# A fused recurrent-attention and expert layer on one Trainium2 core: the first eight steps' log rows come from TensorE, and the last half expert's rows are written over batches finished without them

## The reference, cut to what matters

```python
xn = _layernorm(x)                                   # x: 8 batches x 512 tokens x 256
s  = _L0_attn_ref(xn, ...)
g  = _silu(_L0_ffn_ref(xn, ...))
return x + s * g

# attention, for each batch, chunks of 128 tokens, 16 heads of 16
q, k, v = silu(xn @ Wq.T), silu(xn @ Wk.T), xn @ Wv.T
lf = cumsum(log_sigmoid(xn @ Wf.T + delta))          # within each chunk: "lb" below
o_inter = (q * exp(lb)) @ S
A = (q @ k.T) * exp(where(tril, lb_i - lb_j, -inf))
o = o_inter + A @ v
S = exp(tot) * S + (k * exp(tot - lb)).T @ v
s = (o * rsqrt(mean(o * o) + 1e-6) * norm_weight) @ Wo.T

# experts: 8 experts, each takes its top 128 tokens of every batch
gating, idx = top_k(softmax(xn @ gate_w.T).T, 128)
h = silu(x_in @ w_gate.T) * (x_in @ w_up.T)
out.at[idx].add(gating * (h @ w_down.T))
```

## Time and profile before

| | us |
|---|---|
| median of 3 runs (837.76 to 840.04) | 838.71 |
| the profiled execution, its own time | 838.68 |
| its span in the profile | 836.9 |
| PE busy | 783.8 (94%) |
| DVE, ACT, POOL busy | 541.6, 508.7, 413.8 |

### The profile page before, as it was taken

The page is one execution under the profiler, slowest core; times in us unless marked ns, Lnnn a source line. Parts: engine busy times, 40 slices in busy tenths (PEclk is TensorE's granted clock), DMA queues, the critical chain, the costliest instruction groups (busy, mean ns, idle before and its releaser), DMA issues.

```text
span 836.9 us, 17482 instructions
## 1 busy us (share of the span) xinstructions
PE 783.8 (94%) x6460; PEld 678.3 (81%) x6460; DVE 541.6 (65%) x1024; ACT 508.7 (61%) x1184; POOL 413.8 (49%) x362
## 2 busy tenths in 40 slices
PE   7638999999999999999999999999999999999990
PEld 5526788888888888888888888888888888888880
DVE  6885756666566675666556675576556675565567
ACT  5695755766466665666466655665566655655455
POOL 7767636464255616463355626463364625471311
PEclk9778999999999999999999999999999999999995
DMA  8289898676567857676566757576667758670788
GB/s 279 93 284 226 302 372 214 171 197 196 150 155 192 178 178 165 160 196 193 162 148 193 187 167 161 165 195 190 177 145 189 192 165 230 167 179 16 219 254 288
DMA packets 137637, 160.85 MB, mean 192 GB/s; under 512 B 11856, under 2 KB 108624, under 8 KB 137552
## 3 DMA queue, kind: packets, MB, share of 16 engines
q1 hardware_dynamic: 124832, 142.91, 56.3%
q0 software_dynamic: 12288, 16.79, 12.5%
q10 hardware_dynamic: 432, 0.04, 0.0%
HBM read 117.48 MB, written 42.21 MB: 191 GB/s over the span
## 4 chain that ended last, share of the span: by engine, by line
PE 87%; DMA 3%; SPq 2%; POOL 1%; DVE 1%; issue 1%; ACT 1%; ACTq 0%; DVEq 0%; POOLq 0%
PE y_ps L1699 22%; PE g_ps L1666 21%; PE up_ps L1666 21%; PE m_ps L1542 5%; PE a_ps L1614 4%; PE o_ps L1650 3%; PE m_ps L1596 3%; PE m_ps L1560 2%; PE m_ps L1589 2%; DMA qk_dram<-qk_r 1%; PE o_ps L1639 1%; PE m_ps L1570 1%; SPq L739 1%; DMA ffn_dram<-y_sb,idx_all 1%; DMA w_raw<-w_experts 1%; SPq L695 1%
## 5 line engine op out<-in xcount | busy, mean ns | idle before, releaser
L1666 PE MATMUL up_ps<-xgt,w_r 128*128 128x512 f32 (+1 forms) x792 | 205.8, 395 | 0.0
L1699 PE MATMUL y_ps<-w_r,hid_r 128*128 128x256 f32 x1536 | 205.1, 282 | 0.7 <-DVE hid_r L1493 0.7
L1666 PE MATMUL g_ps<-xgt,w_r 128*128 128x512 f32 (+1 forms) x792 | 201.0, 389 | 3.3 <-ACT xgt L1046 1.8
L1699 PEld LDWEIGHTS y_ps<-w_r,hid_r 128*128 128x128 f32 x1536 | 192.5, 190 | 1.4 <-DVE hid_r L1493 1.0
L1467 DVE SCALAR_TENSOR_TENSOR sg<-sg,g_ps 128x512 f32<-128x512 f32 x123 | 84.2, 684 | 159.9 <-ACT sg L1211 159.9
L887 POOL TENSOR_TENSOR w_r<-w_raw,w_r 128x768 fp32r<-128x768 f32 x64 | 123.1, 1925 | 103.3 <-ACT w_r L1111 103.1
L1666 PEld LDWEIGHTS up_ps<-xgt,w_r 128*128 128x128 f32 x792 | 140.2, 188 | 26.8
L1666 PEld LDWEIGHTS g_ps<-xgt,w_r 128*128 128x128 f32 x792 | 137.7, 189 | 26.1 <-issue 3.6
L1211 ACT ACTIVATE sg<-g_ps 128x512 f32<-128x512 f32 (+1 forms) x132 | 77.1, 584 | 117.0 <-PE g_ps L1666 116.5
L916 POOL DMA_INDIRECT ffn_dram<-y_sb,idx_all x64 | 102.9, 1608 | 64.5 <-DVE y_sb L1369 49.0
L882 POOL TENSOR_SCALAR_AFFINE_SELECT lb_row<-lb_row 128x1024 f32<-128x1024 f32 x62 | 75.8, 1233 | 84.0 <-DMA lb_row<-lb_tiles 83.8
(11 more groups left out here) (246 smaller groups left out, 1021.2 us busy)
## 6 DMA issues: line engine op xcount, KB each, us to landing
lb_row<-lb_tiles SPq DMA_DIRECT2D x62, 512.0 KB, 4.5
w_raw<-w_experts SPq DMA_DIRECT2D x64, 384.0 KB, 3.7
qk_dram<-qk_r SPq DMA_DIRECT2D x32, 512.0 KB, 4.5
k_st<-qk_dram SPq DMA_DIRECT2D x96, 128.0 KB, 3.6
arena<-qk_dram SPq DMA_DIRECT2D x192, 64.0 KB, 3.0
x_all<-x SPq DMA_DIRECT2D x8, 512.0 KB, 9.7
xn_dram<-x_all SPq DMA_DIRECT2D x8, 512.0 KB, 6.6
e_row<-lb_tiles SPq DMA_DIRECT2D x64, 64.0 KB
```

What stands on the lines that cost most here:

```text
L1666: mm = pe.matmul(bank[:, 0:width(n)], w_r[:, m, a, at:at + P], xgt[:, b, k, tokens], start=(j == 0 and k == 0), stop=(j == len(passes) - 1 ...
L1699: mm = pe.matmul(y_ps[:, j, :], hid_r[p][:, a, (j - first_tile) * P:(j - first_tile + 1) * P], w_r[:, m, b, DOWN:DOWN + D], start=(m == 0 ...
```

## The change

It changes both ends of the program. The middle of the loop stays as it is.

**At the start.** The logs of steps 0 to 7 no longer go through DRAM: `spread_logs(t)` on PE writes them into PSUM, one product of an identity with a masked tile (512 columns, with -1e30 above the diagonal) and four fp32 products of 128 columns that spread one row of `lbt` each. `decays(t)` reads PSUM for `t < 8`. `spread_rows(kk)` does the same for batch 0's query rows (four products each), and `rows(0)` moves ahead of the loop. Gone are `load_lb(0..3)`, `mask(0..3)` and `load_rows(0)`. The job ("kt", 0, 0) moves into the loop (`u = 1`), the loads of weight blocks 2 and 3 ahead of SP's loop, `scaled(4)` from ACT to POOL, `out_weights`, two decays and the keys' load forward. ACT makes three constant tiles at the start of `normalise`.

**At the end.** The last half expert is not scattered. Its rows are gathered: of x, of f as the other 15 groups left it, of s (now stored by token) and of r (now also stored to DRAM, as single floats). `row_total` adds the gated result to the gathered f, ACT takes the SiLU, `row_result` finishes the row, and `write_rows` writes it over the row in `out`, after the store of that batch has landed. So batches 4 to 7 are finished first (`FINISH`), beside PE's last steps, and then 0 to 3. The root is taken on DVE alone from a bit-shifted seed with three Newton steps, in two parts (28 tiles, then 4); ACT switches to its SiLU table at `u = TS`.

```diff
-    FIRST = [("k", 0, 0), ("k", 0, 1), ("q", 0, 0), ("q", 0, 1), ("v", 0, 0), ("v", 0, 1), ("kt", 0, 0)]
+    FIRST = [("k", 0, 0), ("k", 0, 1), ("q", 0, 0), ("q", 0, 1), ("v", 0, 0), ("v", 0, 1)]
...
+    FINISH = (4, 5, 6, 7, 0, 1, 2, 3)
+    SOON = 3
+    R_PARTS = (slice(0, (B - 1) * TPB), slice((B - 1) * TPB, NT))
+    ACT_LATE = {TS: ((4, "silu", 0), (4, "silu", 1)), TS + 1: ((5, "weigh", 0), (5, "silu", 0)),
+                TS + 2: ((5, "silu", 1), (6, "weigh", 0)), TS + 3: ((6, "silu", 0), (6, "silu", 1)),
+                TS + 4: ((7, "silu", 0),), TS + 5: ((7, "silu", 1),), TS + 6: ((0, "silu", 0),), TS + 7: ((0, "silu", 1),),
+                TS + 8: ((1, "silu", 0),), TS + 9: ((0, "row", 0), (1, "row", 0)), TS + 10: ((1, "silu", 1),),
+                TS + 11: ((2, "silu", 0),), TS + 12: ((2, "silu", 1), (3, "silu", 0), (3, "silu", 1))}
+    LATE_BETWEEN = {TS + 2: (4, 512, 1024), TS + 5: (6, 0, 256), TS + 6: (6, 512, 768), TS + 7: (6, 768, 1024),
+                    TS + 8: (7, 0, 256), TS + 9: (7, 256, 512), TS + 10: (7, 512, 768), TS + 11: (7, 768, 1024)}
+    DVE_LATE = {TS: ((4, "weigh", 0, 512),), TS + 1: ((4, "weigh", 512, 1024), (4, "add", 0, 512)),
+                TS + 2: ((5, "scaled", 0, 512),), TS + 3: ((5, "scaled", 512, 1024), (5, "add", 0, 1024), (6, "scaled", 0, 512)),
+                TS + 4: ((6, "scaled", 512, 1024),), TS + 5: ((6, "add", 256, 512),), TS + 6: ((7, "weigh", 0, 512),),
+                TS + 7: ((7, "weigh", 512, 1024),), TS + 9: ((0, "rows", 0, 0),), TS + 10: ((1, "rows", 0, 0),),
+                TS + 11: ((0, "weigh", 0, 512),), TS + 12: ((0, "weigh", 512, 1024),)}
...
 sync:
+                def store_r(part):
+                    sp.wait_ge(r_step, R_STEPS * (part + 1))
+                    tiles = R_PARTS[part]
+                    sp.dma_start(r_dram.rearrange("(t p) o -> p (t o)", p=P)[:, tiles], r1[:, tiles],
+                                 allow_slow_non_contiguous=True).then_inc(r_out[part], 16)
...
                 for n in range(2):
                     sp.wait_ge(qk_out[n], 16)
+                load_keys(0)
                 store_part(0, 3)
-                load_keys(0)
+                store_xn(2)
+                load_stacks(0)
                 store_xn(3)
-                load_stacks(0)
+                load_stacks(1)
                 store_lb(1)
-                load_stacks(1)
-                load_rows(0)
+                store_xn(4)
+                sp.wait_ge(d_out, 32)
+                sp.wait_ge(row_exp, 1)
                 for n in range(4, 6):
                     load_lb(n)
+                for n in range(2, 4):
+                    load_weights(n)
...
+                    if u == TS - 4:
+                        store_r(0)
+                    if u == TS - 2:
+                        sp.wait_ge(scattered, 16 * TPB * (2 * E - 2))
+                        for n in FINISH[:SOON]:
+                            fetch_f(n)
...
 gpsimd:
+                def write_rows(t):
+                    pool.wait_ge(o_pair[t // 2], 32)
+                    pool.wait_ge(row_done, 2 * t + 2)
+                    pool.indirect_dma_start(
+                        out=out[:, :], out_offset=bass.IndirectOffsetOnAxis(ap=idx_all[:, E - 1, TPB + t:TPB + t + 1], axis=0),
+                        in_=row_f[t], in_offset=None).then_inc(rows_out, 16)
...
+                    if u == TS - 6:
+                        for t in range(TPB):
+                            gather_rows(row_x, x, t, row_in_soon)
+                    if u == TS - 4:
+                        pool.wait_ge(scattered, 16 * TPB * (2 * E - 2))
+                        for t in range(TPB):
+                            gather_rows(row_f, ffn_dram, t, row_in_soon)
+                    if u == TS - 2:
+                        ...
+                        pool.wait_ge(r_out[0], 16)
+                        for t in range(TPB - 1):
+                            gather_rows(row_s, s_dram[0:(B - 1) * N, :], t, row_in_soon)
+                            gather_rows(row_r, r_dram[0:(B - 1) * N, :], t, row_in_soon)
+                    if u == TS + 4:
+                        ...
+                        gather_rows(row_s, s_dram, TPB - 1, row_in_late)
+                        gather_rows(row_r, r_dram, TPB - 1, row_in_late)
+                    if u == TS + 9:
+                        write_rows(0)
+                        write_rows(1)
...
 scalar:
                 sums(0)
+                act.wait_ge(attn_in[2], 32)
+                out_weights()
+                evacuate(FIRST[3])
                 split(FIRST[2])
-                evacuate(FIRST[3])
-                scaled(2)
+                gates_ratio(1)
+                decays(0)
                 split(FIRST[3])
+                decays(1)
                 evacuate(FIRST[4])
                 evacuate(FIRST[5])
+                scaled(2)
                 scaled(3)
-                act.wait_ge(attn_in[2], 32)
-                out_weights()
-                decays(0)
-                decays(1)
+                decays(2)
+                decays(3)
                 sums(1)
-                for t in range(2, DECS):
-                    decays(t)
+                decays(4)
+                rows(0)
...
 vector:
+                def row_total(t):
+                    dve.wait_ge(dn_done, XQ + MID if t < 2 else XS)
+                    dve.scalar_tensor_tensor(out=row_f[t], in0=y_ps[:, t, :], scalar=gate_all[:, E - 1, TPB + t:TPB + t + 1],
+                                             in1=row_f[t], op0=ALU.mult, op1=ALU.add).then_inc(row_sum, 1)
+                def row_result(t):
+                    dve.wait_ge(row_silu, t + 1)
+                    dve.scalar_tensor_tensor(out=row_f[t], in0=row_f[t], scalar=row_r[t], in1=row_s[t],
+                                             op0=ALU.mult, op1=ALU.mult).then_inc(row_done, 1)
+                    dve.tensor_tensor(row_f[t], row_f[t], row_x[t], ALU.add).then_inc(row_done, 1)
...
-                gated(2 * E - 1, range(2, TPB))
-                add_tokens(1)
-                ...
+                row_total(2)
+                row_total(3)
+                add_tokens(0, slice(0, 512))
+                row_result(2)
+                row_result(3)
+                add_tokens(0, slice(512, 1024))
+                for f in (1, 2):
+                    for h in range(2):
+                        weigh(f, slice(h * 512, (h + 1) * 512))
                     add_tokens(f)
                 for h in range(2):
                     at = slice(h * 512, (h + 1) * 512)
-                    weigh_scaled(B - 1, at)
-                    add_tokens(B - 1, at)
+                    weigh_scaled(3, at)
+                    add_tokens(3, at)
...
 tensor:
+                def spread_logs(t):
+                    if t == 0:
+                        pe.wait_ge(soft, 6)
+                        pe.wait_ge(lb_turned, 2)
+                    if t >= 2:
+                        pe.wait_ge(e_done, t - 1)
+                    pe.matmul(first_logs(t)[:, :], one_r, shut_r.unsqueeze(1).broadcast_to([P, G4, P]), start=True, stop=False,
+                              skip_group_check=True)
+                    for j in range(G4):
+                        r = t * G4 + j
+                        mm = pe.matmul(first_logs(t)[:, j * P:(j + 1) * P], ident[:, r:r + 1].broadcast_to([P, P]),
+                                       lbt[0][:, 0, :], start=False, stop=True, skip_group_check=True)
+                    mm.then_inc(spread_done, 1)
...
                 sums(0)
+                spread_logs(0)
+                spread_logs(1)
                 make(FIRST[4])
                 make(FIRST[5])
-                make(FIRST[6])
+                spread_logs(2)
+                spread_logs(3)
                 sums(1)
+                spread_logs(4)
+                for kk in range(KD):
+                    spread_rows(kk)
+                for t in range(5, FREE):
+                    spread_logs(t)
```

More of the change, by code:

```diff
@@ L37 @@
 TOPK_ROUND = 8
+MASKED = -1e30
 def f32(ap):
@@ L846, in _ @@
                         sp.wait_ge(m_done, order["x", E - 1, 3] + 1)
-                        for n in range(F_EARLY):
+                        for n in FINISH[SOON:]:
                             fetch_x(n)
                     if u == TS + 3:
+                        fetch_s(FINISH[SOON])
+                        store_r(1)
                         sp.wait_ge(scattered, 16 * TPB * (2 * E - 1))
@@ L904, in gather, with scatter @@
                             .then_inc(first_in[t] if (e, half) == (0, 0) else gathered, 16)
-                def scatter(n, tiles=range(TPB)):
+                def scatter(n):
                     e, half = n // HALVES, n % HALVES
@@ L1017, in _ @@
                         scaled(6)
-                scatter(2 * E - 1, range(2, TPB))
-                for t in range(TPB):
-                    pool.wait_ge(last_out[t], 16)
+                write_rows(2)
+                write_rows(3)
```

(28 more changed lines are left out.)

386 lines of the change are left out of this document (220 added, 166 removed).

## The result

The changed kernel takes **852.4 us** (median of 4 runs, 850.6 to 855.3) against 838.2 before: ratio 1.0166, 95% interval 1.0149 to 1.0183. It is slower by 14 us, outside of the predicted range and on the other side. Its profiled execution took 853.89 us, its span 852.2.

The account below looks back on a forecast made before the run. PE was taken to bound the middle, so only its arrival at the unbroken work, hold-ups in the last steps and the 22.0 us tail could move the end. 838.7 less 0.7 (start) and 3.4 (tail) gave 834.6 us, range 831 to 841.

Parts of the forecast that it names:

- the price of `store_r`: Near the end, r's store of 3584 single floats: 3.4 to 13.4 us plus 2, landing at 764 to 775.
- The new POOL queue: Before the last steps: 18 gathers of 1.3 us fit POOL's idle 21.16 us; the last six end by 783, in time.
- last steps: PE's final steps, with finishing work between them: DVE's lateness makes PE end 1.7 us later, at 816.6; bounds 0 and 3.
- Rival 3: Slow single floats: `store_r(0)` lands at 788, PE's squares wait, 12 lost and 4.1 won, 846.6 us; chance 0.12.
- the forecast of 834.6: Whole program: 0.7 won at the start and 3.4 at the end, from 838.7 us; chance 0.48 for 832.7 to 837.
- The start: Before the unbroken PE work: loop begins at 64.4, `gate(1)` at 85.1 against 85.8, 0.7 us won; bounds 1.9 won, 4.1 lost.
- Rival 1: At the start, half clock through the whole spread: loop begins at 69.2, start loses 4.1, 839.4 us; chance 0.17.
- over-full steps: `TS + 2` and `TS + 3`: 9.2 us of DVE work against 4.24; `down(123)` some 0.5 late, `down(124)` 0.8 more.
- rival 2: DVE doesn't hold PE up in the last steps and the clock is full: 7.0 won, 831.7 us; chance 0.17.
- The tail: After PE's last product: DVE needs 13.1 us, ends at 829.7; last store 3.75; span ends at 833.5, 3.4 us won.

Follow-up runs that it names:

- r by partition: Changed kernel with r stored by partition (pieces of 112 and 16 bytes) in place of single floats, and a matching gather index: 845.87 us, repeated unchanged at 843.98.
- fifth group: Three kernels repeated unchanged on chip 10: r by partition 843.98 us, the changed kernel 852.85, x later 846.06.
- shifted: r by partition with 96 repeats of a satisfied wait on PE and 48 on ACT near their start: 833.36 us, ratio 0.9938.
- third group: Chip 13: shifted 833.36 us; x later with the same repeated waits 834.00; x later with the old start 833.42; changed kernel with x loads at TS 851.91.
- fourth group: Chip 3: changed kernel with repeated waits 854.88 us; shifted with r's first part as floats 847.51, last part 852.00; r by partition, waits on ACT only 846.92.
- run with floats and later loads: Changed kernel, single-float stores kept, with the loads of x moved from TS - 2 to TS: 851.91 us, ratio 1.0152.
- x later: r by partition with the three 512 KB loads of x moved from TS - 2 to TS: 831.70 us on chip 15, 846.06 on chip 10.

## Why the prediction was wrong, point by point

The sum by stretches, in us of the profiled executions ("r by partition" is the fifth group's run, of the first kind of chip; "shifted" the third group's, of the second kind):

| | before | changed | r by partition | shifted |
|---|---|---|---|---|
| up to ACT's `gate` at `u = 123` | 750.9 | 753.0 | 751.5 | 751.7 |
| three steps | 15.6 | 25.0 | 26.3 | 15.6 |
| from there to PE's last product | 48.5 | 59.0 | 49.6 | 49.3 |
| tail | 22.0 | 15.2 | 15.2 | 15.2 |

**The first step that failed** is the price of `store_r`: "3.4 to 13.4 us, and 2 to land ... lands at 764 to 775". The bound came from the packets of loads: 3584 x 60 ns over 16 engines. Such a store took 18.5 to 20.1 us to land in the four traces that show its landing, and in the changed kernel the gather behind it starts at 779.80, 18.2 us after its issue. The count was right: q1 has 130352 packets with floats and 126512 with r by partition, 3840 more, which is 4096 floats less 256 pieces. So the Trainium skill's rule of one descriptor for each element ("DMA: Bandwidth & Descriptors", Rules for kernel authors) agrees with the trace. Its 10.5 ns a packet (Measured), which it states for loads, gives an estimate of 38 us for this store; that is nearer than my lower bound, though 1.9 times too much. The late landing by itself cost the changed kernel nothing: the six gathers ended at 787.0 and not by 783, but `add_squares(31)` waited for ACT until 792.09, and PE has no wait at the squares.

What I left out altogether is that the store slows what stands behind it and around it, and the second, seven times smaller store, which the text never costed. That one costs most (5.1 us against 0.6 in the fourth group), since `fetch_f(0)` is issued 0.6 us behind it (811.02, 811.62) and ACT stands waiting for it from 815.3. In all, the floats cost 8.9 us on chip 10 (852.85 - 843.98) and 17.9 on chip 13. In 815 to 821 of the changed kernel, and in 797 to 803 of the shifted one, where the same loads run without floats:

```profile
DMA packets 488, 0.49 MB, mean 81 GB/s; under 512 B 13, under 2 KB 488, under 8 KB 488
...
q1 hardware_dynamic: 488, 0.49, 133.3%
```
```profile
DMA packets 1921, 1.77 MB, mean 295 GB/s; under 512 B 192, under 2 KB 1921, under 8 KB 1921
...
q1 hardware_dynamic: 1921, 1.77, 90.8%
```

That is 6 x 16 x 1.333 / 488 = 0.26 us for each packet against 0.045: a packet of 1 KB takes six times as long behind the floats as without them. These two ran on chips of different kinds; in the fifth group, on one chip, the same 6 us (from 4 us after the store's issue) give 0.21 against 0.05, four times.

**The second step that failed** is a term that I put at nothing. Under "The new POOL queue" the early gathers are priced by POOL's own time alone, and the 1.7 us of the last steps hold DVE's operations alone; for what gathers and loads in flight do to PE and ACT there is no term. On a chip of the second kind that was right (15.6 us for three steps before and after). On those of the first kind, where the changed kernel ran, it is short by 9 to 13 us: 25.0 to 28.5 in place of 15.6. What stops the engines there is open. (The count of 18 gathers is wrong too: the kernel has 16, 14 of them early.)

**Rival 3** named one of the two causes, at 0.12 and with 846.6. Its road (six gathers, `add_squares`, squares) carries nothing in the changed kernel and 3.7 us in the run with floats and later loads, so it is luck that its number is only 6 us too low.

**Without floats** the forecast of 834.6 meets 833.4 on a chip of the second kind (834.0 and 831.7 with x later), and misses 844.0 and 845.9 on two of the first. No row of the trace before, itself of the second kind, could show the latter. And the meeting is in part luck: by the table the start lost 0.8 us where 0.7 were to be won, the last steps lost 0.8 and not 1.7, and the tail won 6.8 and not 5.1; the three errors of 0.9 to 1.7 us nearly cancel.

**The start** was forecast to win 0.7. The loop's first job starts at 61.64 (forecast 64.4), `gate(1)` at 85.71 (85.1). PE stood at full clock longer than I gave it (0.87 on the mean in 49 to 62), then fell to 0.69. Side by side it loses: 1.6 us alone, 1.5 with the end (845.87 - 844.42), 0.6 in the third group (834.0 - 833.4). Alone that is just clear of noise (ratio 1.0002 to 1.0022). What I had not seen is a wait later on. Each of the 16 traces with the new start has, once or twice in 100 to 735 us, PE waiting 0.6 to 2.0 us in all for the queries; none of the four with the old start has it. That of the changed kernel:

```profile
388.23 0.63 ACT L1157 ACTIVATE qk_r<-qs 128x512 fp32r<-128x512 f32 x1 [4.82 <-DMA qk_dram<-qk_r]
...
391.43 0.64 PE L1725 MATMUL m_ps<-v_pad,kd 128*32 128x128 f32 x16 [1.63 <-DVE qs L1375]
```

Why that store is late there I did not try. Rival 1 (half clock) did not come.

**The last steps** were to lose 1.7. From `u = 123` to the end of PE's last product it was 64.0 before, and it is 64.8 in the shifted run: 0.8 lost. DVE holds PE for 1.2 us in two waits, and 0.7 of it, at the last product (813.89 before), was there before: it is this wait that I had read as standing ahead of `down(123)`. So the over-full steps cost 0.5 where I had 1.3; the bound "0 if DVE's operations overlap more" was nearer, and rival 2 had this half right.

**The tail** The earlier trace rows was sized well: 13.1 forecast from PE's end to DVE's, 12.6 measured in both the changed kernel and the shifted one (816.5 to 829.1), and the last store 2.6 in place of 3.75. The tail is 6.8 us shorter, 5.1 were forecast.

## What to carry to other kernels

Price a store by its pieces and never as an event by itself: ask what is issued behind it, and who waits for that. Lay the tensor out so that each partition writes one run, and put the arithmetic into the index; here two small tensors and seven short DVE operations win 9 us on one chip and 18 on another. And before an edit is given the credit of ten microseconds, run it beside its own base on one chip: four edits of mine each "mended" a hole that only the other chips had.

## What was not expected of the hardware

Single floats of 4 bytes: 3584 take 20.1 us to land, 512 take 11.7, so the price is far from proportional. Two chips differ by 14 us (1.7%) on one and the same kernel (831.70 and 846.06), while on the kernel before they differ by 1.7 us (838.07 and 839.73). The best version, r by partition, won 0.5% to 0.7% on chips of one kind (shifted, or with the loads later, or both) and lost 0.5% to 0.8% on the other, where the kernel before stays the fastest.
